# A graph-attention edge loop on one core: two broadcast operands of VectorE moved from SBUF to PSUM

## What is computed

```
h = xn @ W                                   # per node, 8 heads x 32
a1, a2 = (h * attn_l).sum(-1), (h * attn_r).sum(-1)
e = leaky_relu(a1[src] + a2[dst], 0.2)
ex = exp(e - seg_max[dst])
denom = segment_sum(ex, dst)
out = segment_sum(h[src] * (ex / denom[dst])[:, :, None], dst)
```

## Time and profile before

| what | value |
|---|---|
| median of three runs | 3406.3 us |
| span of the profiled execution, first to last instruction | 3357.5 us |
| TensorE busy | 2396.9 us, 71% |
| VectorE busy | 1666.8 us, 50% |
| GpSimd busy | 1856.6 us, 55% |
| ScalarE busy | 614.4 us, 18% |
| mean granted TensorE clock | 0.833 |
| the edge loop, first gather to last step | 130.9 to about 2903 us |

### The profile page before, as it was taken

How to read it: one execution, slowest core, us unless ns; L and a number is a source line. 1 busy time by engine, 2 the same in 40 slices (tenths; PEclk the granted TensorE clock), 3 DMA queues, 4 the chain that set the end, 5 groups by cost and what they waited for, 6 DMA issues and landing times.

```text
span 3357.5 us, 47799 instructions
## 1 busy us (share of the span) xinstructions
PE 2396.9 (71%) x13450; PEld 1756.6 (52%) x13451; DVE 1666.8 (50%) x3416; ACT 614.4 (18%) x1640; POOL 1856.6 (55%) x1764
## 2 busy tenths in 40 slices
PE   4666776766677767666767666676778765379998
PEld 2554455545555555554545445554555554347776
DVE  6544445544445454544545445454555554733334
ACT  2411111111111111111111111011111111043332
POOL 3366666666666666666666666666666676200000
PEclk9878887878788777877878778888888887789999
DMA  6533333333333333333333333333334333100000
GB/s 193 200 99 88 89 96 93 96 97 92 91 96 93 92 97 92 89 94 92 91 97 96 93 91 101 100 99 96 109 106 109 109 94 84 39 29 19 19 19 20
DMA packets 150658, 302.18 MB, mean 90 GB/s; under 512 B 36163, under 2 KB 88347, under 8 KB 150620
## 3 DMA queue, kind: packets, MB, share of 16 engines
q0 software_dynamic: 82848, 233.35, 25.9%
q1 hardware_dynamic: 66100, 66.77, 6.1%
q10 hardware_dynamic: 1672, 1.59, 0.2%
HBM read 269.29 MB, written 32.29 MB: 90 GB/s over the span
## 4 chain that ended last, share of the span: by engine, by line
PE 43%; another core or an unknown queue 22%; DVE 16%; issue 12%; DVEq 2%; ACT 2%; POOL 2%; DMA 0%; ACTq 0%; SPq 0%; POOLq 0%
PE bank L872 16%; PE bank L985 5%; DVE work L1264 4%; PE bank L881 4%; PE bank L824 4%; PE bank L975 4%; DVE acc L1271 3%; PE bank L890 2%; PE bank L836 2%; PE bank L879 2%; POOL work L548 2%; PE bank L785 1%; DVEq L1256 1%; DVE zb L1245 1%
## 5 line engine op out<-in xcount | busy, mean ns | idle before, releaser
L548 POOL DMA_INDIRECT work<-h_tab,idx x1712 | 1809.5, 1057 | 949.9 <-issue 517.8
L872 PE MATMUL bank<-work 128*128 128x264 f32 x3424 | 1039.3, 452 | 420.1 <-DVE work L1264 293.0
L872 PEld LDWEIGHTS bank<-work 128*128 128x128 f32 x3424 | 717.2, 222 | 587.4 <-issue 366.7
L1271 DVE TENSOR_TENSOR acc<-bank,acc 128x264 f32 x856 | 369.0, 431 | 772.3 <-PE bank L872 313.0
L1264 DVE TENSOR_TENSOR work<-work 128x1024 f32<-128x1024 f32 x428 | 508.1, 1228 | 42.1 <-issue 33.9
L647 ACT CAST work<-bank 128x512 bf16<-128x512 f32 x428 | 237.7, 589 | 687.3 <-PE bank L824 427.4
L653 ACT ACTIVATE work<-zb 128x64 f32<-128x64 f32 x214 | 54.9, 256 | 1576.1 <-DVE zb L1249 1179.2
L1245 DVE TENSOR_TENSOR zb<-work,bank 128x64 f32<-128x64 f32 x214 | 47.0, 220 | 528.6 <-remote 489.5
L824 PEld LDWEIGHTS bank<-ident,work 128*128 128x128 f32 x1712 | 259.3, 172 | 92.2 <-issue 80.6
L824 PE MATMUL bank<-ident,work 128*128 128x128 f32 x1712 | 289.5, 321 | 20.9 <-issue 20.6
L836 PEld LDWEIGHTS bank<-a2p,work 128*128 128x128 bf16 x5136 | 203.5, 99 | 152.9 <-issue 114.3
(11 more groups left out here) (236 smaller groups left out, 1883.2 us busy)
## 6 DMA issues: line engine op xcount, KB each, us to landing
work<-h_tab,idx POOLq DMA_INDIRECT x1712
xx_d<-acc SPq DMA_DIRECT2D x49, 256.0 KB, 2.1
xnt_c<-xx_d SPq DMA_DIRECT2D x66, 128.0 KB
h_tab<-acc SPq DMA_DIRECT2D x49, 132.0 KB, 1.9
xn_c<-xx_d SPq DMA_DIRECT2D x49, 128.0 KB
q2t_d<-q2t_c SPq DMA_DIRECT2D x49, 128.0 KB
X<-x SPq DMA_DIRECT2D x6, 1024.0 KB, 11.7
out<-wqkv SPq DMA_DIRECT2D x16, 384.0 KB, 2.6
```

What stands on the lines that cost most here:

```text
L548: nc.gpsimd.indirect_dma_start(out=ring[q][:, j, :], out_offset=None, in_=h_tab, in_offset=bass.IndirectOffsetOnAxis(ap=idx[:, q, j:j + 1] ...
L872: ins = mm(bank[3 + s % 2][:, 0:TW], hot[q][:, s * G + g, :], ring[q][:, s * G + g, :], start=(g == 0), stop=(g == G - 1))
L1271: v.tensor_tensor(a, bank[3 + s % 2][:, 0:TW], a, ALU.add).then_inc(added, 1)
```

## The change

Bank 2 of PSUM gets two tenants beside the picked values. Columns 128 to 191 (`pk_ex`) hold a batch's exponentials, and columns 256 to 383 (`iota_b`) hold a copy of the row of node numbers, made once before the loop. The multiplications and the one-hot comparison read these in place of the SBUF copies. ScalarE now takes the exponential twice, first into `pk_ex`, then into the ring, where TensorE needs it for the denominators; a new semaphore `den_ready` tells of the second. TensorE waits for it before step 0. Before the pick for b+1 TensorE also waits until the one-hots of b+2 are done (`hot_ready` at b+3). GpSimd's wait is as it was.

```diff
+        pk_ex = bank[2][:, TB * AW:TB * AW + TB * H].rearrange("p (j h) -> p j h", h=H)
+        iota_b = bank[2][:, 2 * P:3 * P]
...
+        den_ready = sem("den_ready")
...
                 act.wait_ge(u_ready, b + 1)
-                nc.scalar.activation(ring[q][:, :, C:TW], zb[:, q, 0, :].rearrange("p (j h) -> p j h", h=H),
-                                     ACT.Exp).then_inc(ex_ready, 1)
+                u = zb[:, q, 0, :].rearrange("p (j h) -> p j h", h=H)
+                nc.scalar.activation(pk_ex, u, ACT.Exp).then_inc(ex_ready, 1)
+                nc.scalar.activation(ring[q][:, :, C:TW], u, ACT.Exp).then_inc(den_ready, 1)
...
                     if s % 2 == 0:
                         pe.wait_ge(msg_ready, b * 2 + s // 2 + 1)
+                    if s == 0:
+                        pe.wait_ge(den_ready, b + 1)
                     if s == 2 and not last:
+                        pe.wait_ge(hot_ready, b + 3)
                         pick(b + 1, (q + 1) % R3)
...
-                v.tensor_tensor(hot[q], iota_p[:].unsqueeze(1).to_broadcast([P, TB, P]),
+                v.tensor_tensor(hot[q], iota_b.unsqueeze(1).to_broadcast([P, TB, P]),
                                 dstT[:, bass.ds(b * TB, TB)].unsqueeze(2).to_broadcast([P, TB, P]),
                                 ALU.is_equal).then_inc(hot_ready, 1)
...
+            own(v.tensor_copy(iota_b, iota_p[:]))
...
-                    ex = ring[q][:, k * 4:k * 4 + 4, C:TW].unsqueeze(3).to_broadcast([P, 4, H, HC])
+                    ex = pk_ex[:, k * 4:k * 4 + 4, :].unsqueeze(3).to_broadcast([P, 4, H, HC])
                     v.tensor_tensor(m, m, ex, ALU.mult).then_inc(msg_ready, 1)
```

## The result

The changed kernel takes 3655.93 us in the median of four runs (3642.08 to 3662.68). The kernel before, run beside it, takes 3404.61 (3398.58 to 3411.7). The ratio is 1.0736, 95% interval [1.0705, 1.0766]. The forecast was 3311 us, with a range up to 3440: wrong in sign and outside its range. Of the rivals it was nearest to "TensorE's chain takes over", with more lost than I had priced.

What follows compares the result with a forecast made beforehand. No engine full: a loop of waits, with GpSimd's gather streams budgeted at 12.9 us per batch, not proven to set the pace. Gain 119 us, loss 24, sum -95: 3406.3 - 95 = 3311 us, range 3215 to 3440.

Steps and rivals of the forecast that it cites:

- TensorE's chain takes over: Rival, chance 0.22: pick behind one-hots, add(0) and step 0 sets the pace, slower; 3457 to 3509 us.
- The gathers: GpSimd's gathers: mean falls from 1057 to about 950 ns, maximum to about 1.2 us; 185 us of stretching removed.
- The two operations: VectorE's multiplications and one-hots reading one operand from PSUM: priced at nothing, bounds -13 to +32 us.
- The skill's rule: Trainium skill's inference: two-SBUF-input tensor_tensor leaves descriptor generation's write side alone, so the gathers gain nothing.
- 3430 us: Time if the skill's inference holds: nothing gained at the gathers and only the waits remain.
- my bounds of 27 us either way: ScalarE's exponential into PSUM: taken as 256 ns as into SBUF; half less or more gives -27 to +27 us.
- 0.64 x 185 = 119 us gained: GpSimd's stretching removed, times the share of batches (138 of 214) where VectorE's exponents wait for the unnamed releaser.
- nothing moves: Rival, chance 0.1: gathers stay stretched, or the freed time turns into GpSimd idle time between streams; 3406 us.
- the rows don't prove the cause: Caveat on the reading that a running GpSimd stream delays TensorE's completions until its end; no size given.
- 25 x 0.96 = 24 us lost: TensorE's pick starting 0.96 us later, counted only in the 25 batches where VectorE waited for it by name.
- The cover: TensorE's later pick hides where release is tied to the stream's end: 5.3 us minus 0.86 from pick, 3.4 from step 3.
- my upper bound of 205 us: Upper bound for TensorE's new wait before the pick: 0.96 us lost in all 214 batches.

Runs made afterwards that it cites:

- e3: The changed kernel with only the exponentials in PSUM, node numbers back in SBUF, no wait before the pick: 1.0131 of the kernel before.
- e1: The changed kernel with the node numbers in PSUM bank 7 and no wait before the pick: 3408.86 us, 1.0150 of the kernel before.
- e10: Both operands in PSUM, node numbers in bank 7, no wait before the pick, on another chip: 3442.91 us, 1.0064 of the kernel before.
- e5: Both operands in PSUM, no wait before the pick, GpSimd waiting per step of batch b-3: 2738.4 us, 0.9222 of the kernel before.
- e6: The kernel before, with GpSimd waiting for each step of batch b-3 instead of all four: 2969.25 us, 1.0002 of the kernel before.
- e4: The changed kernel with the pick's tile numbers loaded into TensorE's registers ahead of the wait: 3582.66 us, 1.0639 of the kernel before.
- e2: The kernel before with only TensorE's new wait ahead of the pick, operands left in SBUF: 3595.68 us, 1.0681 of the kernel before.
- e9: The changed kernel unedited, run again on another chip: 3648.25 us, 1.0663 of the kernel before.
- e12: The kernel before with only the new wait ahead of the pick, on another chip: 3661.06 us, 1.0701 of the kernel before.
- e15: The changed kernel unedited, run once more on another chip: 3593.13 us, 1.0711 of the kernel before.
- e11: Both operands in PSUM, no wait before the pick, GpSimd waiting per step, on a slow chip: 3464.2 us, 1.0123 of the kernel before.
- e8: The kernel before with SyncE loading the ring by plain loads, no gathers on GpSimd, output not the reference's: 2341.35 us, 0.7885 of before.
- e17: The kernel before with two 770 ns memsets on GpSimd behind each batch's fourth gather: 3309.7 us, 0.9682 of the kernel before.

## Why the prediction was wrong

**The gathers** came as forecast: 950 ns, 183.7 us less. The two operations cost nothing, 1218 against 1228 ns and 1215 against 1217 ns. The longest gather is 1707 ns and not 1.2 us; a few are still stretched.

**The skill's rule.** By "SBUF — State Buffer", section "Who interferes with whom", of the Trainium skill, a `tensor_tensor` would not have held the gathers. This case decides against that reading for these gathers: one operand moved in both operations, and nearly all the stretching was gone (950 ns; e3, with one of the two operations moved, 991 ns). Why it was so is not settled: the gathers take their row numbers from `idx` in SBUF, and the same section has a VectorE instruction with two SBUF inputs meet GpSimd instructions that read SBUF. No run parts this reading from the making of descriptors. But 3430 us, which I had worked out from it, lay nearer to the result than my forecast, since its gain of nothing came true for another reason. That was luck.

**ScalarE.** The exponential into PSUM takes 228 ns against 256 into SBUF. That is 0.028 x 214 = 6 us less, well inside my bounds of 27 us either way; no run tests it by itself.

**The first step that failed** is "0.64 x 185 = 119 us gained". The share of batches that wait for the unnamed releaser was read as the share in which a shorter stream passes on. e1 and e10 are the change without the wait and measure +47.7 and +17.5 us, so nothing is gained. The freed time became idle time between the streams, which I had as "nothing moves". On the chip of e5 and e6 the gathers lose 231.7 us and the time 230.9, all of it. The term had no size of its own: it depends on what holds the release, and my own reading that a running stream holds it ("the rows don't prove the cause") should have gone into the sum instead of standing beside it.

**The second step that failed** is "25 x 0.96 = 24 us lost". It measures 234.5 and 235.7 us alone and 205.3 beside the rest. Three things are in it, and the runs don't part their shares: 205 to 236 us are 1.0 to 1.1 us per batch. The cover was false: I hid the wait behind the stream's end in 189 batches, but steps 2 and 3 stand behind the pick, GpSimd's next stream stands behind step 3, and so the stream's end moves with it. Counted over all batches, my upper bound of 205 us was about the price, though the next two things were not in it. The delay was mis-sized too: the pick starts 0.83 us *behind* the one-hots' end, where I had it start with that end. Of this 0.5 us is what it does with registers behind the wait (e4 starts at 0.33), and winning these back brought hardly any time. And all picks are now long ones, 356.6 / 214 = 1.67 us against 219.8 / 214 = 1.03. Both of its lengths stood in the earlier trace rows, 1.62 and 0.75 us; I had not asked which one a pick behind a wait takes. e4 moves the register load alone and leaves the length at 1.67.

**The rival** named this place and this order, and its condition, a chain longer than a stream with its gap, was met in nearly every batch instead of half of them: in the changed kernel GpSimd stood before 168 + 32 = 200 of 214 streams for a step by name or an unnamed releaser, 166 before. It gave 3457 to 3509 us; the result is 3656. Adding 205 to 235 us to 3404.61 gives 3610 to 3640, and the 0.6 to 1.5% of e1 and e10 bring it to 3630 to 3690.

**Open.** What in a chip makes it of one kind or the other, and what of the gathers holds TensorE's completions (the issuing, or the transfers that it starts), wasn't settled; the pauses speak for the issuing. That it is TensorE's completions that are held is argued from what the waiting engines wait for, as the profile does not name the releaser. The changed kernel never met a chip of the fast kind. The lower granted clock belongs to the result (0.79 to 0.81 in e2, e9, e12 and e15 as well, 0.83 to 0.84 in e1 and e10), and its share in the 7% wasn't separated.

## What to carry to other kernels

When a buffer's new tenant forces a wait on an in-order engine, price it in every batch, with the register work and the instructions queued behind it, and only then look for cover; here another bank (e1) made the wait needless. Before counting freed time as gained, ask what releases the next stage: if the releaser has no name and comes at the end of another engine's burst, try pauses in the burst first, several short ones. Measure on several chips, with the kernel before on each: the same kernel (e5 and e11) gained 7.8% on one and lost 1.2% on another.

## What the runs showed of the hardware

With GpSimd issuing indirect gathers one behind the other, engines that wait for TensorE went on late, for a releaser without a name, on every chip but the one of e5 to e8: in e1 mostly 1.80 us behind the stream's last gather. The kernel before takes 3361 to 3425 us on those chips and 2968 us on that one; without the gathers on GpSimd it is 2352 and 2341 us.

On the slow chips pauses of 770 ns in the stream, filled with memsets, brought the time down. Adding 163 to 488 us of useless work left the kernel 1.6 to 5% faster than before; the plainest case is e17, the kernel before with 321 us of memsets, 3.2% faster. On the fast chip one such pause cost 131.6 us.

On the fast chip the gathers are the kernel's pace. They take 1084 ns in the mean, stretched beside VectorE's operations with both operands in SBUF, and 948 with one operand of these in PSUM.
